# Two decoder layers on one core: the third phase cut into nine chains, with a softmax that sums and divides its weights before the values

## The reference, cut to what matters

```python
qkv = x @ w_qkv
q, k, v = ...                      # (b, 16 heads, 128, 16)
att = q @ k^T / sqrt(16)
att = where(causal, att, -inf)
att = softmax(att)                 # exp(att - max) / sum
y = att @ v                        # heads side by side: (b, 128, 256)
x = x + y @ w_proj
```

## Time and profile before

| what | value |
|---|---|
| median of three runs | 4092.33 us |
| the profiled execution | 4099.57 us, its span 4097.9 us |
| PE busy | 3883.6 us (95%) |
| DVE busy | 3196.7 us (78%) |
| ACT busy | 2703.6 us (66%) |
| GpSimd (POOL) busy | 2256.6 us (55%) |
| granted TensorE clock, mean | 0.98 |

### The profile page before, as it was taken

One profiled execution on the slowest core, in us unless ns is written; L12 is line 12 of the kernel. 1 busy time (PEld: TensorE's weight loads), 2 busy tenths in 40 slices (PEclk: granted clock), 3 DMA queues, 4 the chain that ended last, 5 costly groups with the idle time before them and its releaser, 6 DMA issues.

```text
span 4097.9 us, 118221 instructions
## 1 busy us (share of the span) xinstructions
PE 3883.6 (95%) x34966; PEld 3044.6 (74%) x34967; DVE 3196.7 (78%) x8792; ACT 2703.6 (66%) x6962; POOL 2256.6 (55%) x2996
## 2 busy tenths in 40 slices
PE   5999999999999999979969999999999999999997
PEld 4888888888888888867756666666667666666665
DVE  5898888888888888835547778788787787787785
ACT  4877878888888778734436666566566566666564
POOL 4656666666656556612225555555555555555554
PEclk9999999999999999979989999999999999999999
DMA  4443333333333333324410101101101101111100
GB/s 130 134 134 112 127 121 116 114 116 112 106 105 115 113 115 109 100 89 143 144 46 26 35 28 31 33 27 31 33 27 32 32 27 35 29 29 31 31 27 21
DMA packets 222642, 304.14 MB, mean 74 GB/s; under 512 B 57216, under 2 KB 176256, under 8 KB 222592
## 3 DMA queue, kind: packets, MB, share of 16 engines
q1 hardware_dynamic: 197632, 249.83, 19.6%
q0 software_dynamic: 19200, 52.45, 4.0%
...
...
## 4 chain that ended last, share of the span: by engine, by line
PE 56%; issue 16%; POOL 10%; ACT 9%; DVE 6%; ACTq 1%; DMA 1%; DVEq 1%; POOLq 0%; another core or an unknown queue 0%; SPq 0%
PE Q L1517 17%; PE Q L1522 10%; PE Q L1510 7%; PE Q L1887 3%; PE Q L1920 3%; PE Q L1739 3%; PE Q L1551 3%; POOL arena L650 3%; PE Q L1560 2%; PE Q L1545 2%; PE Q L1751 2%; POOL arena L658 2%; ACT arena L1325 1%; POOL arena L655 1%; ACT arena L1322 1%
## 5 line engine op out<-in xcount | busy, mean ns | idle before, releaser
L1522 PE MATMUL Q<-ident,arena 128*128 128x128 f32 x3872 | 620.6, 283 | 124.4 <-ACT arena L1251 36.1
L1522 PEld LDWEIGHTS Q<-ident,arena 128*128 128x128 f32 x3872 | 442.7, 142 | 301.6 <-issue 128.4
L650 POOL TENSOR_TENSOR arena<-arena 128x1024 f32<-128x1024 f32 x256 | 482.1, 1905 | 39.9 <-DMA arena<-cum_rows 39.3
L1517 PE MATMUL Q<-Wkvl,arena 128*128 128x512 f32 x1024 | 499.6, 600 | 0.0
L715 POOL TENSOR_TENSOR l<-l,half_pow 128x8 f32<-128x8 f32 x192 | 318.8, 1661 | 230.6 <-DVE l L1130 229.0
L740 POOL TENSOR_TENSOR arena<-arena,part_of 128x512 f32<-128x512 f32 x256 | 264.1, 1043 | 193.9 <-DVE part_of L1168 193.9
L1361 ACT ACTIVATE arena<-Q,mx 128x128 f32<-128x128 f32 x1024 | 287.3, 386 | 104.5 <-DVE mx L945 102.7
L1510 PE MATMUL Q<-arena,Win 128*128 128x128 f32 x2560 | 346.6, 280 | 1.3 <-DVE arena L875 1.3
L1510 PEld LDWEIGHTS Q<-arena,Win 128*128 128x128 f32 x2560 | 323.1, 196 | 5.8 <-DVE arena L875 1.8
L899 DVE TENSOR_TENSOR arena<-arena,Q 128x1024 f32<-128x1024 f32 x256 | 312.0, 1219 | 11.5 <-ACT arena L1316 4.2
L1551 PEld LDWEIGHTS Q<-ident,arena 128*128 128x128 f32 x2048 | 244.1, 145 | 97.4 <-issue 65.8
...
## 6 DMA issues: line engine op xcount, KB each, us to landing
arena<-cum_rows SPq DMA_DIRECT2D x256, 512.0 KB, 6.3
arena<-routed_rows SPq DMA_DIRECT2D x144, 128.0 KB, 2.0
expert_rows<-arena POOLq DMA_DIRECT2D x144, 128.0 KB, 2.0
arena<-in_x_dram SPq DMA_DIRECT2D x128, 128.0 KB, 5.6
arena<-in_ctx_dram SPq DMA_DIRECT2D x128, 128.0 KB, 4.0
x_rows<-arena SPq DMA_DIRECT2D x128, 128.0 KB, 1.7
arena<-x_rows SPq DMA_DIRECT2D x128, 128.0 KB, 2.2
...
```

The source lines that it names most:

```text
L650: tell(g.tensor_tensor(E8[j], E8[j], cums[:, 8 * j:8 * j + 8].unsqueeze(2).broadcast_to([P, 8, T]), ALU.subtract), "diff")
L1517: last = mm(out, lhs(c), rhs(c), start=c == 0, stop=c == n - 1)
L1522: last = nc.tensor.transpose(out[:, c * P:(c + 1) * P], src[:, c * P:(c + 1) * P], ident[:, :])
```

## The change

- **Chains.** A is split into A (gather, norm, q, k, v) and S (scores to projection), K into K and H (latent half of keys and values), L into L (scores, exponentials) and R (turns, values), T into T (projection, norm) and U (quantised layer). Offsets: A 0, S 1, K 2, C 3, H 3, L 3, R 4, T 4, U 5. There are now 69 bodies: 5 partial ones at the start, 59 full ones, 5 partial at the end. New chains share semaphores with chains of phase 1.
- **Strips.** All four strips run at once, strip 3 in Q[5], which L and R use too. The strips wait for R's last read of Q[5], and L's first scores wait for all four groups of exponentials.
- **Exponentials.** All 16 heads get an ACT exponential of 128 columns with the sum taken by the same instruction; DVE's subtractions (L793) and the 512-column exponentials go.
- **Division.** DVE takes four reciprocals of four sums; GpSimd multiplies each strip (128 x 512) by them before the turn.
- **Values.** V1 becomes 32 columns wide for each head, zero in the half that belongs to the neighbour. Each 32-column group accumulates a pair of heads, so the output comes out transposed: 32 instructions. The ACT copy L1436, the four transposes of OT, `headout` and the two transposes of oT go.
- **x3c.** ACT copies x3 to x3c (128 x 256), which the final addition reads one body later.
- **values() of phase 1** runs in two pairs of strips instead of four single ones, in rotation over four column groups instead of two at a time.
- **ORDER.** New orders for all engines of phase 3; phase 1 loses the tokens Ppv1 and Ppv3.

```diff
     3: {
         "SP": """
-            Ax Cc Kx Lm Tx To
+            Cc Tx Lm Ax Uo Kx
         "POOL": """
-            Ag Kx4c Kln5 Aln4 Kln6 Clnc Tlno Tln7 Klq1 Lp0 Lp1 Lp2 Clq0 Lp3 Klq2
+            Clnc Uln7 Kx4c Ag Kln5 Hlq2 Sp0 Sp1 Clq0 Sp2 Kln6 Sp3 Tlno Aln4 Klq1 Lp0 Lp1 Lp2 Lp3
         "DVE": """
-            Kln5 Clnc Ax3 Aln4 Kln5n Kln6 Aln4n Lmr Kln6n Tlno Clncn Tx5 Tln7 Lm0 Lm1 Taq Klq1 Ak Lm2 Lm3 Lp0 Lp1 Klu1 Am0 Am1 Am2 Am3 Lp2 Tx6 Clq0 Lp3 At0 Lt0
-            At2 Klq2 Clu0 Lt2 Aho Klu2 Ax4
+            Lmr Clnc Uln7 Rt0 Clncn Kln5 Rt2 Uaq Sm0 Hlq2 Sm1 Ux6 Sm2 Sm3 Sp0 Kln5n Hlu2 Sp1 Clq0 Kln6 Sp2 Clu0 Ax3 Kln6n Sp3 St0 Lm0 Lm1 Tlno Aln4
+            St2 Aln4n Klq1 Lm2 Lm3 Tx5 Lp0 Klu1 Lp1 Lp2 Sx4 Ak Lp3
         "ACT": """
+            Rt1 Hlq2 Clncn Rt3 UaT Sm0 Sm1 Clq0 Rlo HlT2 Sm2 Sm3 ClT0 Hla4 Kln6n Lp0 Lp1 St1 St3 Klq1 SoT Aln4n Lp2 Lp3 KlT1 Aq Cla3 Ac
         "PE": """
-            Two Twoh Aln4n Ls0 Kln6n Aq Clncn Kla0 Kla0h Aqv Ak Cla1 Ls2 TaT As0 Ttern KlT1 Cla1h Lt0 As3 Lt1 Kla2 At0 At1 Kla2h At2 At3 Apv Apv0 Apv1 Apv2 Apv3
-            Lt2 Lt3 AOT Lpv0 AoT ClT0 KlT2 Apr Lpv1 Cla3 Cla3h Kla4 Kla4h
+            Rt0 Hla2 Rt1 Rt2 Hla2h Rt3 Clncn Ss0 UaT Cla1 Utern Cla1h Rpv0 Rpv1 HlT2 St0 Two Hla4 Hla4h St1 ClT0 St2 Ls0 Kln6n Twoh St3 Kla0 Kla0h Ls2
+            Spv Spvh Aln4n Cla3 Spr Aq Aqv Ak KlT1 Cla3h
...
@@ block.gpsimd @@
+            def S(b):
+                for j in range(4):
+                    yield f"p{j}"
+                    done(pool, "rc1", b, j + 1)
+                    tell(g.tensor_tensor(S1[:, j, :, :], S1[:, j, :, :], rc1[:, 4 * j:4 * j + 4].unsqueeze(2).broadcast_to([P, NG, T]), ALU.mult), "P1n")
...
@@ block.vector @@
+            def S(b):
+                banks = (Q[0], Q[1], Q[2], Q[5])
+                for j in range(4):
+                    yield f"m{j}"
+                    done(dve, "S1", b, j + 1)
+                    tell(v.tensor_reduce(mx1[:, 4 * j:4 * j + 4], banks[j][:, :].rearrange("p (g k) -> p g k", g=NG), AX.X, ALU.max, negate=True), "S1max")
+                for j in range(4):
+                    yield f"p{j}"
+                    done(dve, "P1", b, j + 1)
+                    was(dve, "P1n", b, 4)
+                    tell(v.reciprocal(rc1[:, 4 * j:4 * j + 4], den1[:, 4 * j:4 * j + 4]), "rc1")
...
@@ block.scalar @@
+            def S(b):
+                banks = (Q[0], Q[1], Q[2], Q[5])
+                for j in range(4):
+                    yield f"m{j}"
+                    done(act, "S1max", b, j + 1)
+                    for g in range(NG):
+                        h = 4 * j + g
+                        last = s_.activation(S1[:, j, g, :], banks[j][:, g * T:(g + 1) * T], ACT.Exp, bias=mx1[:, h:h + 1], accum_out=den1[:, h:h + 1])
+                    tell(last, "P1")
...
@@ block.tensor @@
             def values(b, bank, PT, V, n, by="vsvs"):
-                for j in range(4):
-                    yield f"pv{j}"
-                    done(pe, f"PT{n}{by[j]}", b, by[:j + 1].count(by[j]))
-                    for g in range(NG):
-                        h = 8 * (g // 2) + 2 * j + g % 2
-                        last = mm(bank[32 * (h % 4):32 * (h % 4) + AW + 1, h // 4 * T:(h // 4 + 1) * T], V[:, h, :], PT[:, j, g, :], start=True, stop=True)
+                for first in (0, 2):
+                    yield f"pv{first}"
+                    for j in (first, first + 1):
+                        if j > first or by[first] != by[first + 1]:
+                            done(pe, f"PT{n}{by[j]}", b, by[:j + 1].count(by[j]))
+                    for half in (0, 2):
+                        for j in (first, first + 1):
+                            for g in (half, half + 1):
+                                h = 8 * (g // 2) + 2 * j + g % 2
+                                last = mm(bank[32 * (h % 4):32 * (h % 4) + AW + 1, h // 4 * T:(h // 4 + 1) * T], V[:, h, :], PT[:, j, g, :], start=True, stop=True)
...
@@ block.tensor, chain S, from step s0 @@
+                if not isinstance(b, int) or b >= 3:
+                    done(pe, "PTlv", b + (-3), 2)
+                strips(b, banks, (0, 1, 2, 3), QT1, KT1, 1, mask)
                 for j in range(4):
                     yield f"t{j}"
-                    if j < 3:
-                        done(pe, "P1", b, j + 2)
-                    else:
+                    if j == 3:
                         done(pe, "PT1v", b)
-                    turn(b, Q[(1, 2, 0, 1)[j]], S1, j, 1)
+                    done(pe, "P1n", b, j + 1)
+                    turn(b, Q[j % 3], S1, j, 1)
                 yield "pv"
-                done(pe, "PT1s", b)
-                yield from values(b, Q[2], PT1, V1, 1)
-                yield "OT"
-                done(pe, "OT1", b)
-                tell(transposes(Q[0], S1[:, 0, :, :].rearrange("p g q -> p (g q)"), NG), "PV1")
-                yield "oT"
-                done(pe, "o1", b)
-                tell(transposes(Q[1], o1, DC), "oT1ps")
+                done(pe, "PT1s", b, 2)
+                done(pe, "PT1v", b, 2)
+                for c in range(DC):
+                    if c:
+                        yield "pvh"
+                    for k in range(2):
+                        for j in range(4):
+                            h = 8 * c + 2 * j + k
+                            last = mm(Q[1][32 * j:32 * j + 32, c * T:(c + 1) * T], V1[:, h, :], PT1[:, j, 2 * c + k, :], start=k == 0, stop=k == 1)
+                tell(last, "PV1")
...
@@ block.tensor, chain L, step s0 @@
+                if not isinstance(b, int) or b + 2 < NB:
+                    done(pe, "P1", b + 2, 4)
                 scored((0, 1))
...
-            program(pe, "PE", 3, (("A", A, 0), ("C", C, 1), ("K", K, 1), ("L", L, 2), ("T", T_, 3)))
+            program(pe, "PE", 3, (("A", A, 0), ("S", S, 1), ("C", C, 3), ("K", K, 2), ("H", H, 3), ("L", L, 3), ("R", R, 4), ("T", T_, 4), ("U", U, 5)))
```

More of the change, by code:

```diff
@@ L105, in two_layers, with signals @@
         SEM, PER, BASE = {}, {}, {}
-        def signals(chain, engine, names):
-            sem = ctx.enter_context(nc.semaphore(f"{chain}_{engine}"))
+        ended = {}
+        def signals(chain, engine, names, after=""):
+            if after:
+                sem, begun = ended[f"{after}_{engine}"]
+            else:
+                sem, begun = ctx.enter_context(nc.semaphore(f"{chain}_{engine}")), 0
             total = 0
@@ L321, in two_layers @@
             sig(n)
-        signals("A", "DVE", "x3 ln4_var ln4_xn k1c S1max:4 PT1v:2 o1 x4")
-        signals("A", "PE", "ln4_Tps qv1 k1 S1:4 PT1ps:4 PV1:2 oT1ps proj1")
-        signals("A", "ACT", "ln4_T q1c v1c P1:4 PT1s:2 OT1 oT1")
+        signals("A", "DVE", "x3 ln4_var ln4_xn k1c")
+        signals("A", "PE", "ln4_Tps qv1 k1")
+        signals("A", "ACT", "ln4_T q1c v1c x3c")
         signals("A", "POOL", "ln4_rstd")
+        signals("S", "DVE", "S1max:4 rc1:4 PT1v:2 x4", after="X")
+        signals("S", "PE", "S1:4 PT1ps:4 PV1 proj1", after="X")
+        signals("S", "ACT", "P1:4 PT1s:2 oT1", after="X")
+        signals("S", "POOL", "P1n:4", after="N")
         signals("C", "DVE", "lnc_var lnc_xn latss0 kn0")
@@ L1113, in A @@
                 tell(v.tensor_copy(KT1, cut(Q[2][:, 0:D], DC)), "k1c")
[L1114 to L1118 removed]
+            def S(b):
[9 more added lines that the diff above has]
+                    tell(v.reciprocal(rc1[:, 4 * j:4 * j + 4], den1[:, 4 * j:4 * j + 4]), "rc1")
+                yield from evac(b, (Q[0], None, Q[2], None), PT1, 1)
                 yield "x4"
```

162 lines of the change are left out of this document (78 added, 84 removed).

## The result

The changed kernel takes 4025.95 us in the median of four runs (4019.42 to 4034.38), the kernel before 4091.94 us beside it: a ratio of 0.9841 (95% interval 0.9826 to 0.9856). It is faster by 66 us where 139 were forecast. The profiled execution took 4028.71 us with a span of 4027.1.

A forecast was written before the change was run, and what follows sets the result against it. PE was taken to bound full bodies (30.28 of 30.60 us busy). 28.08 us of work plus 0.45 waiting gave 28.5; 59 x 28.5 + 200 = 1882 against 2021.2, 139 less: 3953 us forecast, range 3915 to 4030.

The forecast's parts named there:

- PE's work: Phase 3, full body: strips, values and transposes save 2.20 us of PE time, 30.28 falling to 28.08 us.
- The ring: Phase 3, Ak to HlT2: DVE's chain takes 11.45 us against 11.0 of PE work, so PE waits 0.45 us.
- DVE's run to the quantised rows: Phase 3, DVE from Ak: 3.9 us up to Rt2, then a copy of 0.60 and the quantisation of 2.33.
- the forecast body: Phase 3, full body: 28.08 us of PE work plus 0.45 of waiting, 28.5 us; bounds 28.2 to 28.9.
- the latent mask: Phase 3, PE before L's first scores: a wait for ACT's exponentials there would show the forecast wrong; 2.8 us if slow.
- Fill and drain: Phase 3's partial bodies: 140 us of work and some 60 idle, 200 us; bounds 185 to 225.
- a lock and small waits: Phase 3, x3 beside POOL's Sp2: DVE and POOL block each other, up to 1.04 us a body; 4012 us, chance 0.23.
- ACT's sums: Phase 3: exponentials with sums don't overlap, 0.59 us each, PE waits 2.8 us a body; 4119 us, chance 0.07.
- a gain in phase 1: Phase 1's values: they speed up too, about 34 us less; 3919 us, chance 0.03.
- strips not side by side: Phase 3: four strips don't run together, 1.2 us comes back, body 29.5 us; about 4012 us, chance 0.04.
- PE alone: Phase 3: DVE finishes its run 0.45 us sooner, body 28.08 us, 25 us less; 3928 us, chance 0.13.

The follow-up runs named there:

- h4: Changed kernel with phase 1's values and their two tokens as before the change; ratio to the kernel before 0.9852, body 29.66 us.
- g2: Changed kernel with plain transfers of fixed blocks for the gathers by index (another output); ratio to the kernel before 0.9818, body 29.07 us.
- g4: Changed kernel with one more 512-column reduction on DVE ahead of the mask row; ratio to the kernel before 1.0005, body 30.33 us.
- h2: f2 with DVE doing ln5's moments right behind the quantisation, ahead of Sm0; ratio to the kernel before 0.9866, body 29.45 us.
- h3: h2 with plain transfers of fixed blocks for the gathers by index (another output); ratio to the kernel before 0.9859, body 29.38 us.
- k1: Changed kernel with the moments of ln5 and ln7 moved ahead of Ak, to the body before; ratio to the kernel before 0.9811, mean body 29.17 us.
- f2: Changed kernel with context keys normalised ahead of Sp1, ClT0 ahead of St1, Hlu2 ahead of ln5's norm; ratio to the kernel before 0.9806.
- f4: Changed kernel with the edits of f2 and f3 together; ratio to the kernel before 0.9834, body 29.33 us.
- f3: Changed kernel with ln5's moments on DVE behind Sm0 and Hlq2, its root on GpSimd behind Hlq2; ratio to the kernel before 1.0012.
- e3: Changed kernel with PE making chain A's keys before its values; ratio to the kernel before 0.9862, body 29.63 us.
- e1: Changed kernel unedited, yardstick on its chip; ratio to the kernel before 0.9846, body 29.58 us.
- g1: f2 with ln5's moments on DVE behind x6 and f3's order on POOL; ratio to the kernel before 0.9944, body 29.98 us.

## Why the prediction had the direction and missed the size

**PE's work: right.** Values 1.01 us (1.03 forecast), mask and strips 1.35 (1.36), PE busy 27.79 in a body (28.08). Exponentials 0.34 us apart (0.36). Phase 1: nothing (h4).

**The ring: the right mechanism, too short.** The forecast let 11.45 us pass from Ak to HlT2, with 11.0 of PE work. Measured are 3022.24 - 3010.43 = 11.81 us with 11.81 - 0.79 - 0.25 = 10.77 of work. (The forecast's own terms add up to 11.3 and 10.9; rounding raised both alike.) That adds 0.36 us to a body. The part that was mis-sized is DVE's run to the quantised rows: 7.31 us for the 3.9 + 0.60 + 2.33 = 6.83 of the forecast. 0.23 of the 0.48 is the clamp, at 0.53 instead of 0.30; g2, which took the gathers away, gave this back. Of the rest 0.16 lies ahead of the copy of Rt2 (4.06 for 3.9) and 0.08 in the other operations of the quantisation. That DVE's run sets the pace is shown by g4 (more work: longer), by h2 against h3 (PE earlier: nothing) and by the mask row, within one profile (0.83 more in the run, 0.79 more in the body). And k1's 28.65 us show that the forecast body can be had with the same work.

**A wait that was overlooked.** The forecast named the latent mask as a place where it could be wrong, for the exponentials. It waits for something else: ACT's copy of the turned context keys (L1482), which needs 0.6 us behind ClT0, and only one turn, 0.5 us, stands between ClT0 and Ls0 in PE's order. 0.43 us in each body. I had followed the context keys up to ClT0 and not beyond. f2 moved ClT0 up and had the wait away, for one of 0.37 us at St2.

Together: 28.53 + 0.36 + 0.43 - 0.10 (PE's work outside the ring: 29.23 - 1.47 - 10.77 = 16.99 for 28.08 - 11.0 = 17.08) = 29.22 us, a usual body of the profile after (29.23). The mean of 29.34 has three bodies of 30.02 in it, with the lock at the mask row, and one of 32.9. There GpSimd stood idle for 3.54 us ahead of its second gather (3691.75 us); what follows on GpSimd came late, and PE waited 2.4 us at HlT2. The kernel before has the same once (3.64 us, at 3788.6), so the change did not bring it.

**Fill and drain: a term mis-sized.** The idle time came out near by luck: PE is busy for 84.50 + 78.31 = 162.8 of 219.4 us, idle for 57 (60 forecast). Before, it was 154.3 - 106.1 = 48, not the 63 that the forecast kept. And the busy time was taken as 5 x 28.08 = 140. In these stretches the granted clock is 0.83 and 0.89 on average, between the levels of 1.2 and 2.4 GHz, and the work of a body takes longer. (An estimate: 84.50 x 0.83 + 78.31 x 0.89 = 139.8 us at full clock, next to 5 x 27.79 = 139.) The earlier trace rows had it: 68.08 + 38.01 = 106 us busy for three bodies of 30.28 = 91. I had put those 15 us down to idle time, as a constant; with five bodies they became 24.

**The rivals.** The one nearest to the result is that of a lock and small waits (4012 us, 0.23 of the chance): 4026 lies within 14 us of it and 73 from the forecast. But it is near by its size and not by its means, which is luck. It put the lock at x3, where L1122 keeps to 0.48 us as changed (and takes 1.15 in every body of f2, the fastest of its set, and of f4). As changed the lock is small (0.8 us at the mask row in 3 bodies of 48; the clamp's 0.23 beside the gather may be of the same kind, which no run shows); it decided f3 and most bodies of k1, and took back most of e3's earlier start. One of the two keeps its time and the other ends behind it: in k1 at 2667.98 us GpSimd starts first and keeps 1.04; in the profile after, at 3011.20, both start at once by the trace, the mask row keeps to 0.29 and GpSimd's product takes 1.19 instead of 1.04. The Trainium skill (SBUF — State Buffer, Who interferes with whom) says that whoever issues first has the shared ports for the whole instruction; and it names tensor_scalar, in its two-port modes, beside the forms with two SBUF inputs. The prediction left that form out, though the mask row and the clamp are of it. The trace agrees on both for the product and the mask row. For the gather it doesn't show a hold over the whole instruction: the clamp inside its first part kept to 0.29 us. ACT's sums (0.07), a gain in phase 1 (0.03), strips not side by side (0.04) and PE alone (0.13) did not come.

**Open.** What the stall in the strips is. It appears on some chips only and in neither kernel without gathers by index, and PE goes on 0.38, 0.43 and 0.45 us (medians) after the second gather's end in e1, g1 and h2. What it waits for the profile doesn't show. Whether the kernel before has it on those chips no trace tells; its medians there are 4103 to 4107 us, for 4085 to 4092 on the others.
